# Graph attention streams: one PSUM bank for the weights, five or four for the slot sums, and an earlier place for two of the weighing steps

## The chip, the cores and the metric

The kernel runs on one core of a Trainium2 chip. The metric is the device time of one execution in microseconds; lower is better. A run's time is compared with others of the same kernel; the median of three runs is given.

## The reference

Two layers of a graph network over 6250 nodes with 256 features and 106250 edges (50000 random pairs in both directions, and a loop at each node), sorted by the node they lead to:

```
x = x + gat0(xn, edges) + mix0(xn)      # xn = layernorm(x)
x = x + moe0(layernorm(x))
x = x + gat1(xn, edges) + mix1(xn)      # gat1: two attention rounds, 4 heads, then 1
x = x + moe1(layernorm(x))
```

The change touches the three attention rounds (8, 4 and 1 heads). Each of them is

```
e     = leaky_relu(a_src[src] + a_dst[dst])
alpha = exp(e - max of e over the edges with this dst) / their sum
out   = sum over the edges with this dst of alpha * h[src]
```

## The kernel before

**Tiling.** The edges lie in slots of 256, which belong to one block of 128 nodes each; a slot has two units of 128 edges. There are 464 slots and 928 units, the same in all three rounds. Eight slots, 16 units, are a group; a round is a stream of 58 groups. `stream_sync`, `stream_gpsimd`, `stream_vector`, `stream_tensor` and `stream_scalar` issue it, one for each engine, each in an order written out by hand; semaphores join them. The mixers, the experts and the preparation of the edges lie outside the streams, but for `Out1`, the output part of the second layer's mixer, whose steps are hooked in between the steps of the second stream (`side.after_scores`, `side.before_carry` with L1970, `side.before_reference`, `side.after_weigh3` with L1987 and L1989, and so on). In the first and third stream `Alone` does nothing there. `Out1` uses PSUM bank 3.

**One group.** GpSimd gathers the row h[src] of each of 128 edges with one indirect DMA a unit (L978) into a ring of 48 units, three groups; it waits for `slot_mm` of the slot that used the place before. For group k, which is one ahead of the group g = k - 1 whose rows are weighed and summed:

- `expand` (TensorE, L1157) brings a_dst to the edges by one-hot matmuls, made by ScalarE's `one_hot` (L1252, L1254).
- `scores` (VectorE, L1008 to L1013) adds a_src and takes the leaky relu. `turn` (TensorE, L1165) transposes the scores, `turned` (ScalarE, L1258) copies them.
- `runs` (VectorE, L1020, L1022) takes running maxima along the edges of a node. `edges` (TensorE, L1169, L1170) brings the ends of the units into one row; `carry` (VectorE, L1030 to L1046) joins them over the units of the group; `cols` (TensorE, L1175) turns the result back; `reference` (VectorE, L1052 to L1056) subtracts the maximum.
- `weights` (ScalarE, L1264) takes exp; `back` (TensorE, L1181, L1182) transposes the result into a PSUM bank of the weights (`BK_W`, two of them, taken in turn); ScalarE copies them (L1266), takes the factor of the rescaling (L1267) and signals `r_ready`.

For group g the weights are there:

- `weigh(g, q)` (VectorE, L1065) multiplies the four units of quad q in place by the weights it reads from `BK_W`, and signals `m_ready`.
- `spread(g, q)` (ScalarE, L1241, L1244) makes the 0/1 matrices of edges against nodes, `Sr`, for the quad, and signals `s_ready`.
- `quad(g, q)` (TensorE, L1194) multiplies them with the rows: for each of its two slots two matmuls into one PSUM bank. The sums of the slots take banks 0, 1 and 2 in turn, and a slot waits until the sum three slots back has been taken (L1191, `slot_added`). The last matmul of a slot signals `slot_mm`.
- `add(s)` (VectorE, L1087) adds the slot's sum to the block's output; `rescale` (L1074) comes before a group's first sum.

**Orders.** VectorE in one turn of the loop: `scores(k)`, weigh 0, the last two sums of the group before, `rescale`, `runs(k)`, weigh 1, sums 0 and 1, `carry(k)`, weigh 2, sums 2 and 3, `reference(k)`, weigh 3, sums 4 and 5. TensorE: `turn(k)`, quad 0, `edges(k)`, quad 1, `cols(k)`, quad 2, `expand(k + 1)`, `back(k)`, quad 3. An engine issues strictly in its order, and each step waits for what it needs. SP brings the masks of group k + 2 when `reference` of group k has signalled `x_ready`. fp32 matmuls stand in the trace as two instructions each, so a quad has eight.

Of the kernel before, what the change touches and what calls it, by code (L numbers as in the profile page):

```python
# [11 lines left out]
ALU = mybir.AluOpType  # L12
ACT = mybir.ActivationFunctionType
# [107 lines left out]
def program(nc, A, out):  # L121
    ctx = ExitStack()
    with ctx:
# [23 lines left out]
        ident = sb("ident", [128, 128])  # L147
# [15 lines left out]
        banks = [ctx.enter_context(nc.psum_tensor(f"ps{i}", [128, 512], F32)) for i in range(8)]  # L163
# [705 lines left out]
        def mix0_gpsimd(e):  # L869
# [24 lines left out]
        assert AR.at <= 25608  # L894
        r_ready, s_ready, m_ready, slot_mm, slot_added, y_clear, den_ready, split_ready, scaled = [
            sem(n) for n in ("r_ready", "s_ready", "m_ready", "slot_mm", "slot_added", "y_clear", "den_ready", "split_ready", "scaled")]
        BK_AD, BK_T, BK_W = banks[4], banks[5], banks[6:8]

        AR.reset()
        Yflat = AR.take(NB * 264)  # L900
# [2 lines left out]
        Sr = AR.take(8, 128)  # L903
# [27 lines left out]
        def g_units(L, u, n):  # L931

            a = u % 48 * L.YW
            return Gflat[:, a:a + n * L.YW].rearrange("p (u h d) -> p u h d", u=n, h=L.H)
# [62 lines left out]
        def stream_vector(e, L, walk, side):  # L997
# [60 lines left out]
            def weigh(g, q):  # L1058

                K = L.k0 + g  # L1060
                if q == 0:
                    e.wait_ge(r_ready, K + 1)
                G = g_units(L, 16 * g + 4 * q, 4).rearrange("p u h d -> p (u h) d")[:, :, 0:D]
                w = BK_W[K % 2][:, 4 * H * q:4 * H * q + 4 * H].unsqueeze(2).to_broadcast([128, 4 * H, D])
                e.tensor_tensor(G, G, w, ALU.mult).then_inc(m_ready, 1)  # L1065

            def rescale(g):
# [9 lines left out]
            def add(s, at):  # L1077
                n = L.s0 + s
                if at is None:
                    at = walk.to(s, YW, WORDS)  # L1080
                o = Yv[:, bass.ds(at, YW)]
                e.wait_ge(slot_mm, n + 1)
                if s % 8 == 0:
                    e.wait_ge(scaled, L.k0 + s // 8 + 1)
                else:
                    e.wait_ge(slot_added, n)
                e.tensor_tensor(o, banks[n % 3][:, 0:YW], o, ALU.add).then_inc(slot_added, 1)  # L1087

            x = ADS[:, 0:NB * H].rearrange("p (b h) -> p b h", h=H)
            parts = AD3[:, 0:NB * L.TS].rearrange("p (b n) -> p b n", n=L.TS)  # L1090
# [9 lines left out]
            for g in range(-1, NG2):  # L1100
                k = g + 1
                more = k < NG2
                if more:
                    scores(k)
                side.after_scores(e, k)
                if g >= 0:
                    weigh(g, 0)
                    if g >= 1:
                        add(8 * g - 2, None)
                        add(8 * g - 1, None)  # L1110
                    at = rescale(g)
                side.before_runs(e, k)
                if more:
                    runs(k)
                if g >= 0:
                    weigh(g, 1)
                if g >= 0:
                    add(8 * g, at)
                    add(8 * g + 1, None)
                side.before_carry(e, k)  # L1120
                if more:
                    carry(k)
                if g >= 0:
                    weigh(g, 2)
                    add(8 * g + 2, None)
                    add(8 * g + 3, None)
                side.before_reference(e, k)
                if more:
                    reference(k)
                if g >= 0:  # L1130
                    weigh(g, 3)
                side.after_weigh3(e, k)
                if g >= 0:
                    add(8 * g + 4, None)
                    add(8 * g + 5, None)
# [8 lines left out]
        def stream_tensor(e, L, walk, side):  # L1144
# [32 lines left out]

            def back(k):
                e.wait_ge(ex_ready, L.k0 + k + 1)
                w = BK_W[(L.k0 + k) % 2]  # L1180
                e.transpose(w[:, 0:P], B2[0:P, :], ident[0:P, 0:P])  # L1181
                e.matmul(w[:, 128:128 + H], OHROW[0:1, :], DD[0:1, 0:H], start=True, stop=True).then_inc(al_ps, 1)  # L1182

            def quad(g, q):
                Q = 4 * (L.k0 + g) + q
                e.wait_ge(s_ready, Q + 1)
                e.wait_ge(m_ready, Q + 1)
                for s in range(8 * g + 2 * q, 8 * g + 2 * q + 2):
                    n = L.s0 + s
                    if n >= 3:  # L1190
                        e.wait_ge(slot_added, n - 2)  # L1191
                    for i in range(2):
                        u = 2 * s + i
                        t = e.matmul(banks[n % 3][:, 0:YW], Sr[:, u % 8, :], GV[:, u % 48, :], start=(i == 0), stop=(i == 1))  # L1194
                    t.then_inc(slot_mm, 1)

            e.wait_ge(split_ready, L.i + 1)
# [32 lines left out]
        def stream_scalar(e, L, side):  # L1230
# [28 lines left out]

            def weights(k):  # L1260
                K = L.k0 + k
                w = BK_W[K % 2]
                e.wait_ge(x_ready, K + 1)
                e.activation(B2[0:P, :], B2[0:P, :], ACT.Exp).then_inc(ex_ready, 1)  # L1264
                e.wait_ge(al_ps, K + 1)
                e.activation(g_units(L, 16 * k, 16)[:, :, :, D], w[:, 0:P].rearrange("p (u h) -> p u h", h=H), ACT.Copy)  # L1266
                e.activation(RR[:, 0:H], w[:, 128:128 + H], ACT.Exp).then_inc(r_ready, 1)  # L1267

            one_hot(0, 0)
            one_hot(0, 1)  # L1270
# [1435 lines left out]
```

## Time and profile before

| what | value |
|---|---|
| median of 3 runs | 6557.96 us (6548.13 to 6566.23) |
| span of the profiled execution, first to last instruction | 6525.8 us |
| what lies around the span in that execution | not among the rows |
| mean granted TensorE clock, share of full speed | 0.796 |
| first, second, third stream, us from the span's start | about 580 to 1915, 2700 to 4235, 4340 to 5715 |
| busy: TensorE matmuls, VectorE, ScalarE, GpSimd | 66%, 54%, 49%, 50% |

How to read it: busy time counts an engine's own instructions, not its waits, register work or DMA issue. "Idle before" is the time the engine stood still just before an instruction, and behind the arrow stands what ended it: an engine with the line of the instruction that released it, "issue" where the profile shows nothing that it waited for, "remote" where the semaphore moved at that moment but no instruction's end is near it. The start of a TensorE row is recorded, its end is modelled. PEclk is the clock granted to TensorE, as a share of 2.4 GHz; its two levels are 1.2 and 2.4 GHz. A row by stretch has: the stretch and its length in us; busy us and instructions of PE (TensorE's matmuls), PEld (its weight loads), DVE (VectorE), ACT (ScalarE) and POOL (GpSimd); PEclk; the DMA engines' busy share; GB/s.

### The profile page before, as it was taken

What the parts mean: (1) busy time and instruction counts of PE and PEld (TensorE: products, weight loads), DVE (VectorE), ACT (ScalarE), POOL (GpSimd) and SP (SyncE); (2) the same over time, 40 slices, a digit from 0 to 9 for tenths busy, and PEclk for the clock granted to TensorE, in tenths of its full rate; (3) what the DMA queues carried; (4) which work ended last, traced back from release to release, by engine and by line L of the source; (5) the groups of instructions that cost most, each with busy time, mean ns of one, the idle gap of its engine ahead of it and who ended that gap; (6) DMA issues with size and microseconds to landing.
All of it is one profiled execution on the core that took longest, in us unless ns stands there. A gap on an engine that the chain in (4) does not pass through costs nothing.

```text
span 6525.8 us, 75215 instructions
## 1 busy us (share of the span) xinstructions
PE 4307.6 (66%) x17795; PEld 2999.8 (46%) x17795; DVE 3511.9 (54%) x10013; ACT 3189.4 (49%) x7093; POOL 3265.5 (50%) x3443
## 2 busy tenths in 40 slices
PE   2896565666653696677676766645555555589798
PEld 2554444444432584355555554434444444433455
DVE  4376565656566437566666666655554545552211
ACT  1365555555542223466666666545555555544222
POOL 0125666666655535355555555546666666501222
PEclk9997777767775798777877778777776677799999
DMA  3292444444431333233333333334444444310110
GB/s 101 63 281 79 122 122 122 121 122 121 123 100 54 103 110 113 80 105 103 105 100 106 101 102 102 96 109 114 113 114 115 113 115 112 97 65 23 33 36 26
DMA packets 347491, 659.78 MB, mean 101 GB/s; under 512 B 78834, under 2 KB 196608, under 8 KB 346664
## 3 DMA queue, kind: packets, MB, share of 16 engines
q0 software_dynamic: 156336, 433.43, 24.1%
q1 hardware_dynamic: 190732, 221.55, 11.6%
q8 instruction: 164, 2.69, 0.2%
q14 instruction: 259, 2.12, 0.1%
HBM read 540.63 MB, written 115.42 MB: 101 GB/s over the span
## 4 chain that ended last, share of the span: by engine, by line
PE 26%; ACT 14%; another core or an unknown queue 13%; issue 7%; DVE 6%; POOL 2%; DMA 0%; DVEq 0%; SPq 0%; POOLq 0%; ACTq 0%
PE ps L1194 6%; ACT AR L1241 4%; PE ps L2560 3%; PE ps L2541 3%; PE ps L2249 2%; ACT AR L1254 2%; ACT AR L1252 2%; ACT AR L1244 2%; PE ps L2046 1%; POOL D_sx L1635 1%; PE ps L1678 1%; PE ps L1669 1%; PE ps L2261 1%; DVE AR L1087 1%
## 5 line engine op out<-in xcount | busy, mean ns | idle before, releaser
L978 POOL DMA_INDIRECT AR<-D_z,SRCI x1856 | 1758.9, 948 | 1231.6 <-issue 490.6
L1194 PE MATMUL ps<-AR 128*128 128x264 f32 (+2 forms) x5568 | 1923.5, 504 | 280.5 <-issue 133.0
L1194 PEld LDWEIGHTS ps<-AR 128*128 128x128 f32 x5568 | 1345.4, 254 | 641.6 <-issue 181.6
L978 POOL DMA_INDIRECT AR<-D_h,SRCI x904 | 865.7, 958 | 458.1 <-issue 242.8
L1241 ACT ACTIVATE AR<-iota_n,NREL 128x128 f32<-128x128 f32 x2784 | 880.9, 389 | 205.4 <-remote 143.9
L1087 DVE TENSOR_TENSOR AR<-ps,AR 128x264 f32 (+2 forms) x1392 | 589.5, 424 | 544.9 <-remote 228.7
L1065 DVE TENSOR_TENSOR AR<-AR,ps 128x1024 f32<-128x1024 f32 x696 | 836.8, 1202 | 6.3 <-ACT AR L1267 6.0
L1244 ACT ACTIVATE AR<-AR,ones 128x512 f32<-128x512 f32 x696 | 502.2, 722 | 22.6
L1266 ACT ACTIVATE AR<-ps 128x128 f32<-128x128 f32 (+2 forms) x174 | 51.1, 294 | 864.9 <-remote 728.3
L1254 ACT ACTIVATE AR<-AR,ones 128x1024 bf16<-128x1024 bf16 x348 | 399.5, 1148 | 11.3
L1252 ACT ACTIVATE AR<-AR,iota_p 128x1024 bf16<-128x1024 bf16 x348 | 394.7, 1134 | 20.3 <-DMA AR<-D_rel 20.3
L1175 PE MATMUL ps<-ones,AR 1*128 1x1 f32 (+2 forms) x696 | 83.1, 219 | 437.8 <-DVE AR L1046 327.6
L1008 DVE TENSOR_REDUCE AR<-ps 128x128 f32<-128x384 f32 (+2 forms) x174 | 64.7, 372 | 509.9 <-remote 496.7
L1165 PE MATMUL ps<-ident,AR 128*128 128x128 f32 (+2 forms) x174 | 60.6, 348 | 382.7 <-DVE AR L1013 335.9
L1052 DVE SCALAR_TENSOR_TENSOR AR<-AR,ps 128x128 f32<-128x128 bf16 (+2 forms) x174 | 60.3, 346 | 457.8 <-remote 431.7
L1175 PEld LDWEIGHTS ps<-ones,AR 1*128 1x128 f32 (+2 forms) x696 | 68.1, 158 | 501.0 <-DVE AR L1046 364.6
L2472 POOL DMA_INDIRECT out<-X x57 | 56.8, 997 | 332.5 <-DVE X L2508 322.3
L1157 PE MATMUL ps<-AD,AR 128*128 x2784 | 165.0, 174 | 83.6 <-issue 43.9
L1165 PEld LDWEIGHTS ps<-ident,AR 128*128 128x128 f32 (+2 forms) x174 | 23.4, 134 | 426.4 <-issue 420.9
L1181 PE MATMUL ps<-ident,AR 128*128 128x128 f32 (+2 forms) x174 | 57.0, 327 | 241.9 <-ACT AR L1264 220.3
L2541 PE MATMUL ps<-AR 128*128 x912 | 200.8, 381 | 18.2 <-ACT AR L2525 18.2
L1264 ACT ACTIVATE AR<-AR 128x128 f32<-128x128 f32 (+2 forms) x174 | 53.3, 306 | 322.9 <-DVE AR L1056 242.1
(437 smaller groups left out, 7814.2 us busy)
## 6 DMA issues: line engine op xcount, KB each, us to landing
AR<-D_rel SPq DMA_DIRECT2D x348, 256.0 KB
D_sx<-AR SPq DMA_DIRECT2D x8, 6370.0 KB
AR<-D_z,SRCI POOLq DMA_INDIRECT x1856
AR<-D_h,SRCI POOLq DMA_INDIRECT x928
D_y<-AR SPq DMA_DIRECT2D x106, 128.0 KB, 1.7
AR<-in_L_ffn_Wd SPq DMA_DIRECT2D x8, 1024.0 KB
AR<-D_mask SPq DMA_DIRECT2D x58, 128.0 KB
D_h<-AR SPq DMA_DIRECT2D x49, 132.0 KB
```

What stands on the lines that cost most here:

```text
L978: e.indirect_dma_start(out=GV[:, u % 48, :], out_offset=None, in_=D_row[L.i], in_offset=bass.IndirectOffsetOnAxis(ap=SRCI[:, u:u + 1], axi ...
L1065: e.tensor_tensor(G, G, w, ALU.mult).then_inc(m_ready, 1)
L1087: e.tensor_tensor(o, banks[n % 3][:, 0:YW], o, ALU.add).then_inc(slot_added, 1)
L1157: t = e.matmul(BK_AD[:, 3 * H * u:3 * H * u + 3 * H], OHr[v][:, 128 * (u % 8):128 * (u % 8) + 128], AD3[:, at], start=True, stop=True)
L1175: t = e.matmul(BK_T[0:P, 384 + i:385 + i], ROW[0:1, i, 0:P], ones[0:1, 0:1], start=True, stop=True)
L1194: t = e.matmul(banks[n % 3][:, 0:YW], Sr[:, u % 8, :], GV[:, u % 48, :], start=(i == 0), stop=(i == 1))
L1241: t = e.activation(w[:, i, :], iota_n[:, :], ACT.Abs, bias=NREL[:, u:u + 1])
L1244: e.activation(w[:, :, :], w[:, :, :], ACT.Relu, bias=ones[:, 0:1], scale=-1.0).then_inc(s_ready, 1)
L1252: e.activation(OHr[v], RBr[n % 2], ACT.Abs, bias=iota_p[:, 0:1], scale=-1.0).then_inc(*ac.up())
L1254: e.activation(OHr[v], OHr[v], ACT.Relu, bias=ones[:, 0:1], scale=-1.0).then_inc(oh_ready, 1)
L2541: t = e.matmul(ps[:, 0:256], rH2[q % 2][:, m, 128 * i:128 * i + 128], Wd[:, m, bass.ds(at, 256)], start=(m == 0), stop=(m == 7))
L2560: t = e.matmul(banks[2 + n % 4][:, 0:w], W1[:, k, 128 * m:128 * m + 128], rxt3[q % 2][:, k, 0:w], start=(k == 0), stop=(k == 1))
```

## The change

The weights keep one bank, 6, for all groups. Bank 7 goes to the sums: the slots of the first and third stream take banks 0, 1, 2, 3 and 7 in turn, those of the second 0, 1, 2 and 7 (bank 3 belongs to the side work). A slot waits for the sum as many slots back as there are banks, and the first slots of a stream wait for none. In VectorE's order weigh 2 moves from behind `carry` to behind weigh 1, ahead of sums 0 and 1; weigh 3 moves from behind `reference` to behind `carry`, where weigh 2 was, ahead of sums 2 and 3. The orders of the other engines, all instructions and their sizes stay.

```diff
--- before.py
+++ after.py
@@ -894,7 +894,13 @@
         assert AR.at <= 25608
         r_ready, s_ready, m_ready, slot_mm, slot_added, y_clear, den_ready, split_ready, scaled = [
             sem(n) for n in ("r_ready", "s_ready", "m_ready", "slot_mm", "slot_added", "y_clear", "den_ready", "split_ready", "scaled")]
-        BK_AD, BK_T, BK_W = banks[4], banks[5], banks[6:8]
+        BK_AD, BK_T, BK_W = banks[4], banks[5], banks[6]
+        SUMS = ((0, 1, 2, 3, 7), (0, 1, 2, 7), (0, 1, 2, 3, 7))
+
+        def sum_of(L, s):
+
+            return banks[SUMS[L.i][s % len(SUMS[L.i])]][:, 0:L.YW]
+
 
         AR.reset()
         Yflat = AR.take(NB * 264)
@@ -1061,7 +1067,7 @@
                 if q == 0:
                     e.wait_ge(r_ready, K + 1)
                 G = g_units(L, 16 * g + 4 * q, 4).rearrange("p u h d -> p (u h) d")[:, :, 0:D]
-                w = BK_W[K % 2][:, 4 * H * q:4 * H * q + 4 * H].unsqueeze(2).to_broadcast([128, 4 * H, D])
+                w = BK_W[:, 4 * H * q:4 * H * q + 4 * H].unsqueeze(2).to_broadcast([128, 4 * H, D])
                 e.tensor_tensor(G, G, w, ALU.mult).then_inc(m_ready, 1)
 
             def rescale(g):
@@ -1084,7 +1090,7 @@
                     e.wait_ge(scaled, L.k0 + s // 8 + 1)
                 else:
                     e.wait_ge(slot_added, n)
-                e.tensor_tensor(o, banks[n % 3][:, 0:YW], o, ALU.add).then_inc(slot_added, 1)
+                e.tensor_tensor(o, sum_of(L, s), o, ALU.add).then_inc(slot_added, 1)
 
             x = ADS[:, 0:NB * H].rearrange("p (b h) -> p b h", h=H)
             parts = AD3[:, 0:NB * L.TS].rearrange("p (b n) -> p b n", n=L.TS)
@@ -1114,21 +1120,19 @@
                     runs(k)
                 if g >= 0:
                     weigh(g, 1)
-                if g >= 0:
+                    weigh(g, 2)
                     add(8 * g, at)
                     add(8 * g + 1, None)
                 side.before_carry(e, k)
                 if more:
                     carry(k)
                 if g >= 0:
-                    weigh(g, 2)
+                    weigh(g, 3)
                     add(8 * g + 2, None)
                     add(8 * g + 3, None)
                 side.before_reference(e, k)
                 if more:
                     reference(k)
-                if g >= 0:
-                    weigh(g, 3)
                 side.after_weigh3(e, k)
                 if g >= 0:
                     add(8 * g + 4, None)
@@ -1177,21 +1181,19 @@
 
             def back(k):
                 e.wait_ge(ex_ready, L.k0 + k + 1)
-                w = BK_W[(L.k0 + k) % 2]
-                e.transpose(w[:, 0:P], B2[0:P, :], ident[0:P, 0:P])
-                e.matmul(w[:, 128:128 + H], OHROW[0:1, :], DD[0:1, 0:H], start=True, stop=True).then_inc(al_ps, 1)
+                e.transpose(BK_W[:, 0:P], B2[0:P, :], ident[0:P, 0:P])
+                e.matmul(BK_W[:, 128:128 + H], OHROW[0:1, :], DD[0:1, 0:H], start=True, stop=True).then_inc(al_ps, 1)
 
             def quad(g, q):
                 Q = 4 * (L.k0 + g) + q
                 e.wait_ge(s_ready, Q + 1)
                 e.wait_ge(m_ready, Q + 1)
                 for s in range(8 * g + 2 * q, 8 * g + 2 * q + 2):
-                    n = L.s0 + s
-                    if n >= 3:
-                        e.wait_ge(slot_added, n - 2)
+                    if s >= len(SUMS[L.i]):
+                        e.wait_ge(slot_added, L.s0 + s - len(SUMS[L.i]) + 1)
                     for i in range(2):
                         u = 2 * s + i
-                        t = e.matmul(banks[n % 3][:, 0:YW], Sr[:, u % 8, :], GV[:, u % 48, :], start=(i == 0), stop=(i == 1))
+                        t = e.matmul(sum_of(L, s), Sr[:, u % 8, :], GV[:, u % 48, :], start=(i == 0), stop=(i == 1))
                     t.then_inc(slot_mm, 1)
 
             e.wait_ge(split_ready, L.i + 1)
@@ -1259,12 +1261,11 @@
 
             def weights(k):
                 K = L.k0 + k
-                w = BK_W[K % 2]
                 e.wait_ge(x_ready, K + 1)
                 e.activation(B2[0:P, :], B2[0:P, :], ACT.Exp).then_inc(ex_ready, 1)
                 e.wait_ge(al_ps, K + 1)
-                e.activation(g_units(L, 16 * k, 16)[:, :, :, D], w[:, 0:P].rearrange("p (u h) -> p u h", h=H), ACT.Copy)
-                e.activation(RR[:, 0:H], w[:, 128:128 + H], ACT.Exp).then_inc(r_ready, 1)
+                e.activation(g_units(L, 16 * k, 16)[:, :, :, D], BK_W[:, 0:P].rearrange("p (u h) -> p u h", h=H), ACT.Copy)
+                e.activation(RR[:, 0:H], BK_W[:, 128:128 + H], ACT.Exp).then_inc(r_ready, 1)
 
             one_hot(0, 0)
             one_hot(0, 1)
```

## Rows read from the trace of the kernel before

**Rows 1.** Busy time by stretch: the first, second and third stream.
```profile
580.00:1915.00 1335.00, 806.30 (x3295) 577.89 (x3295) 816.07 (x1886) 733.38 (x1595) 859.18 (x898) 0.74 0.43 120
2700.00:4235.00 1535.00, 1029.28 (x4405) 761.21 (x4404) 934.90 (x2587) 960.12 (x2095) 874.42 (x923) 0.77 0.37 103
4340.00:5715.00 1375.00, 763.49 (x3338) 551.49 (x3339) 682.45 (x1911) 732.65 (x1620) 869.07 (x918) 0.71 0.40 111
```

**Rows 2.** L1008, `scores`, in the first and third stream: starts, and releasers of its waits.
```profile
L1008 DVE TENSOR_REDUCE AR<-ps x58: 547/557/559, 587.5 to 1904.8; 128x128 f32<-128x384 f32 x58
...
  remote: 171.6, 41
...
L1008 DVE TENSOR_REDUCE AR<-ps x58: 197/207/209, 4341.4 to 5694.2; 128x16 f32<-128x48 f32 x58
...
  remote: 211.5, 30
```

**Rows 3.** Costliest groups, GpSimd's gathers, first, second and third stream.
```profile
L978 POOL DMA_INDIRECT AR<-D_h,SRCI x898 | 859.6, 957 | 455.7 <-issue 241.3 <-remote 165.5 <-PE ps L1194 48.9
...
L978 POOL DMA_INDIRECT AR<-D_z,SRCI x923 | 875.3, 948 | 635.1 <-PE ps L1194 313.4 <-issue 240.9 <-remote 80.8
...
L978 POOL DMA_INDIRECT AR<-D_z,SRCI x918 | 869.3, 947 | 475.5 <-issue 245.7 <-remote 198.3 <-PE ps L1194 31.4
```

**Rows 4.** VectorE in order of time, two groups of the first stream (start, duration).
```profile
1217.96 0.43 DVE L1087 TENSOR_TENSOR AR<-ps,AR 128x264 f32 x1 [3.92 <-PE ps L1194]
...
1223.23 1.20 DVE L1065 TENSOR_TENSOR AR<-AR,ps 128x1024 f32<-128x1024 f32 x1
...
1234.42 0.56 DVE L1008 TENSOR_REDUCE AR<-ps 128x128 f32<-128x384 f32 x1 [5.45 <-remote]
...
1241.48 0.27 DVE L1030 COPY AR<-ps 1x128 f32<-1x128 f32 x1
...
1244.72 1.20 DVE L1065 TENSOR_TENSOR AR<-AR,ps 128x1024 f32<-128x1024 f32 x1
...
1252.11 0.36 DVE L1052 SCALAR_TENSOR_TENSOR AR<-AR,ps 128x128 f32<-128x128 bf16 x1 [5.21 <-remote]
```

**Rows 5.** GpSimd in order of time, the same stretch.
```profile
1223.07 0.94 POOL L978 DMA_INDIRECT AR<-D_h,SRCI  x1 [2.56 <-remote]
...
1234.76 0.94 POOL L978 DMA_INDIRECT AR<-D_h,SRCI  x1 [2.00 <-PE ps L1194]
...
1252.42 0.94 POOL L978 DMA_INDIRECT AR<-D_h,SRCI  x1 [2.67 <-remote]
```

**Rows 6.** TensorE's matmuls in order of time, the same stretch.
```profile
1244.86 0.60 PE L1175 MATMUL ps<-ones,AR 1*128 1x1 f32 x4 [2.16 <-DVE AR L1046]
1246.03 3.04 PE L1194 MATMUL ps<-AR 128*128 128x264 f32 x8 [0.57 <-issue]
```

**Rows 7.** L1052, `reference`: us and times TensorE's release ended its wait, by stream.
```profile
  remote: 81.0, 20
...
  remote: 181.3, 38
...
  remote: 169.4, 26
```

**Rows 8.** Costliest groups, TensorE: L1194 in the three streams, then L1175 in the first.
```profile
L1194 PE MATMUL ps<-AR 128*128 128x264 f32 x1808 | 661.5, 526 | 89.9 <-issue 45.6 <-DVE AR L1065 20.3 <-ACT AR L1244 17.1
...
L1194 PE MATMUL ps<-AR 128*128 128x260 f32 x1821 | 578.9, 474 | 61.4 <-ACT AR L1244 31.3 <-issue 14.0 <-DVE AR L1087 13.7
...
L1194 PE MATMUL ps<-AR 128*128 128x257 f32 x1846 | 659.8, 517 | 126.3 <-issue 71.5 <-ACT AR L1244 43.7 <-DVE AR L1087 7.9
...
L1175 PE MATMUL ps<-ones,AR 1*128 1x1 f32 x228 | 44.7, 296 | 217.1 <-DVE AR L1046 180.6 <-issue 36.5
```

**Rows 9.** Costliest groups, VectorE's side work in the second stream.
```profile
L1970 DVE SCALAR_TENSOR_TENSOR AR<-ps,AR 128x256 f32<-128x256 f32 x49 | 23.4, 477 | 15.5 <-PE ps L2006 8.1 <-remote 7.3
...
L1987 DVE TENSOR_TENSOR X<-X,ps 128x256 f32<-128x256 f32 x49 | 20.6, 420 | 66.9 <-issue 33.9 <-PE ps L2035 30.1 <-remote 3.0
```

## The prediction

> **What bounds the kernel now.** I began with the page and the busy times by stage. The three streams fill 1335, 1535 and 1375 us of a span of 6525.8 us, and no engine is above 68% in any of them [rows 1]. Outside them the change alters no instruction. So I looked for the beat of a stream. The instance rows of the first VectorE step of a group give it: 58 groups whose first and last start at 587.5 and 1904.8 us are 23.1 us apart in the first stream, and in the third (4341.4 to 5694.2) 23.7 [rows 2]; the second's 1535 us are 26.5 a group [rows 1].
>
> The third stream is the telling one. VectorE has 682.45 us of work there against 816.07 in the first [rows 1], 2.3 us a group less, much of it in `carry`, yet its group is no shorter. VectorE's work is not what sets the beat of these two. GpSimd's rows come near it: busy time and the idle time put down to "issue" are 859.6 + 241.3 us for 898 gathers, 1.23 us each, or 19.6 us for the 16 of a group; the other idle time is 165.5 + 48.9 us, 3.7 a group. In the third stream 1.21 us each and 198.3 + 31.4 us give 19.4 + 4.0; in the second the pauses are 313.4 + 80.8 us, 6.8 a group [rows 3]. The gathers stop because they want rings of rows back, which `slot_mm` gives.
>
> Next I read two groups of the first stream in order of time. VectorE stands still three times in them: 3.92 us before the second sum at 1217.96, 5.45 us before `scores` at 1234.42, 5.21 us before `reference` at 1252.11 [rows 4]. GpSimd pauses three times in the same stretch, 2.56, 2.00 and 2.67 us [rows 5]. Each VectorE wait is for TensorE, and longer than TensorE's own rows explain: the `cols` matmuls end by their row at 1245.46 and quad 2 behind them at 1249.07 [rows 6], but `reference`, which needs `cols` alone, starts at 1252.11. TensorE's finished work becomes visible late while gathers are under way, and comes free about when they pause. The reader is to see that most gaps of VectorE are not lack of work on TensorE but this lateness. How common the three are: `reference` waits for TensorE in 20 groups of the first stream and 26 of the third [rows 7], `scores` in 41 and 30 [rows 2].
>
> **Five (four) banks for the sums.** A slot's matmul waited for the sum three slots back. The idle time that TensorE spends before L1194 for L1087 is 13.7 us in the second stream, 7.9 in the third, and in the first under 17.1, the smallest releaser printed [rows 8]. All of it would be under 39 us. Below, the gain is nothing, since most of TensorE's earlier start is eaten by late visibility. I take a quarter-odd, 8 us. A loss I exclude: no bank is shared anew by engines at one time; back(k) writes the one weights bank only after reference(k), which now stands behind weigh 3.
> The Trainium skill (Perfetto Trace Analysis, Optimizing Tensor Performance, Matmuls) says that independent matmul groups should rotate through PSUM banks so that emptying one overlaps filling the next. By that rule alone the whole wait of under 39 us would go; the rows show the rotation already short of binding.
>
> **Weigh 2 goes from behind `carry` to before the first two sums.** One weigh is 1.20 us [rows 4]. What it frees: quad 2 no longer waits for it. In the second of the two groups `carry` gives way to weigh 2 at 1244.72 [rows 4], and quad 2 starts at 1246.03 while `cols` is over at 1245.46 [rows 6]: 0.57 us. TensorE's idle time for L1065 in the first stream is 20.3 us [rows 8]. The gain lies between 0 and 0.57 x 116 = 66 us for the first and third streams; I take 0.3 us in half of the groups, 17 us.
> What it costs: `carry` starts 1.2 us later wherever VectorE wasn't waiting before it. In about half of the groups it was (3.92 us at 1217.96 [rows 4], cover enough). In the others (`carry` at 1241.48 waits for nothing [rows 4]) `cols` is 1.2 us later, and queued behind `cols` on TensorE are quad 2, `expand` and `back`. There the wait before `reference` covers it: 5.21 us. I take 0; if visibility moves with `cols`, the price is 1.2 x 57 = +68 us.
>
> **Weigh 3 goes from behind `reference` to before the next sums.** In groups whose `reference` waits, it is done in the wait, and VectorE, which after 1252.11 [rows 4] has its next steps ready, is 1.2 us ahead: weigh 0, quad 0 and `runs` come 1.2 us earlier. What is late next is the second sum (3.92 us of wait [rows 4]). If that wait ends with a pause of the gathers, the 1.2 us are lost in it; if it ends with its own matmul, they are kept. So 0 to 1.2 x 57 pairs = 68 us; I take half, 34 us. In the other groups weigh 2 plays the same part inside the wait of 1217.96, and the next wait (5.45 us) takes what it gains: 0. ScalarE's exp and `back` wait for `reference`, which is no later there, as one weigh before it replaces another. No DMA moves; SP's masks wait for x_ready, GpSimd for `slot_mm`, and neither is later.
>
> **The second stream** has side work in the same order. Weigh 2 now precedes L1970 too, whose whole wait is 15.5 us in 49 [rows 9], so there is almost no cover before it: L1970 and `carry` are 1.2 us late in every group, 1.2 x 58 = +70 us if nothing hides it. Behind them stands the wait of `reference`, 181.3 us in 38 of 58 groups [rows 7]. Uncovered are some 20 groups: +24 us. After `reference` the freed 1.2 us fall into the wait of L1987 (66.9 us in 49, 1.4 each [rows 9]): no gain. Below nothing isn't excluded, as the pauses of 6.8 us a group may shrink: 0 to +70, I take +24.
>
> **Sum.** -8 - 17 - 34 + 24 = -35 us against the profiled execution: 6525.8 to about 6491. The span lies 32 us (0.5%) under the median of the runs, and no row shows what lies around it; I take the same step from the median: 6558 - 35 = 6523 us.
>
> **The rivals.**
> A, a pause drops out. The first and third streams look locked: three pauses to two groups. 57 pairs, one pause of 2.0 to 2.7 us less in each, about 120 us: 6438. For it: freed VectorE time comes right after a release, when completions are prompt (`scores` at 1234.42 is followed by `carry` at 1241.48 with no wait named [rows 4]). Against: 2.3 us less work in the third stream dropped none.
> B, slower: `carry` becomes the bound. Its place is L1175 behind L1046, where TensorE already idles 180.6 us in the first stream [rows 8]. Price 1.2 us where VectorE arrives at `carry` unhindered: +68 and +70, less 17 + 34 + 8 freed and some of the cover left, about +60: 6618. It decides once more than half of the `reference` waits move with `cols` instead of ending at a pause. For it: the second stream has no cover before `carry`; against: the waits are 3 to 5 us, 1.2 is little.
> The Trainium skill (TensorE: Matmul & The Clock Gate, Why this matters for your kernels) warns that idle gaps between bursts halve TensorE's clock. The granted clock is 0.71 in the third stream and 0.77 in the busier second [rows 1], which agrees; by that rule a longer gap before `cols` would make B dearer, by what no row tells.
> C, nothing moves: the gathers and their pauses set the beat and every 1.2 us sinks into another wait, as between the first and third streams: 6558. The banks not binding at all belongs here.
>
> **How the numbers follow.** Forecast 0.40 (its own range 6483 to 6553, from twice the gain to hardly any), A 0.15, B 0.22, C 0.23. About 0.3% (20 us) is what a measurement can tell from no change. Faster takes A and four fifths of the forecast, 0.47; same C and the rest, 0.31; slower B, 0.22. The range takes in A's 6438 and goes up to just short of B's 6618; half of A and of B may lie beyond: 6435 to 6615.
>
> **What would show it.** Idle time before L1194 for sums near 0 (banks); quad 2 starting when `cols` ends; `reference` waits shorter by 1.2 us in the first and third streams, and the waits before the second sum shorter too; GpSimd's pauses fewer (A), the same (C) or longer (B); TensorE's idle time for L1046 longer by up to 60 us a stream in B. I'd be wrong if the waits before `reference` stay as long as now with `carry` later.

## The result, and the profile after

The changed kernel needs 6599.07 us (median of 20 runs, 6563.23 to 6625.98), the kernel before 6547.66 in the 20 runs beside them (6510.41 to 6588.46). The ratio of after to before is 1.0073, with a 95% interval of 1.0054 to 1.0091: slower by some 48 us, where the forecast was 35 us faster. The new time lies inside the range given, but on the side of rival B. The profiled execution of after took 6616.12 us, its span is 6614.1; that is 17 us above its median, and the one of before shown above lay 20 us under its own, so the two spans overstate the loss.

The busy times by stretch of the changed kernel answer to [rows 1] (columns: stretch, its length, then busy us and instructions of PE, PEld, DVE, ACT and POOL, the granted clock, the DMA share, GB/s):

```profile
580.00:1930.00 1350.00, 806.86 (x3286) 592.24 (x3287) 813.73 (x1871) 729.37 (x1584) 861.03 (x900) 0.72 0.44 119
2700.00:4310.00 1610.00, 1049.20 (x4496) 767.09 (x4496) 955.62 (x2643) 978.83 (x2146) 881.51 (x928) 0.78 0.37 99
4400.00:5800.00 1400.00, 735.55 (x3358) 535.89 (x3356) 698.06 (x1916) 736.23 (x1626) 879.31 (x928) 0.73 0.41 111
```

No engine has more to do: over the whole span TensorE's matmuls are busy 4282 us against 4308 before, VectorE 3524 against 3512. The first line of the answer for `scores` in each stream gives its length as in [rows 2], from the first start to the last:

```profile
L1014 DVE TENSOR_REDUCE AR<-ps x58: 547/557/559, 590.4 to 1928.1; 128x128 f32<-128x384 f32 x58
...
L1014 DVE TENSOR_REDUCE AR<-ps x58: 347/358/359, 2744.5 to 4298.8; 128x64 f32<-128x192 f32 x58
...
L1014 DVE TENSOR_REDUCE AR<-ps x58: 197/208/209, 4420.6 to 5781.8; 128x16 f32<-128x48 f32 x58
```

From 590.4 to 1928.1 are 1338 us, then 1554 and 1361, against 1317, about 1511 and 1353 of before. All three look longer. Only the second is, as the profiles from set 4 below will show; the profile of before shown above came from other conditions. The costliest groups that answer to [rows 8] and [rows 3] (TensorE's quads by stream, then `cols` in the first, then the gathers by stream):

```profile
L1196 PE MATMUL ps<-AR 128*128 128x264 f32 x1808 | 673.3, 536 | 42.0 <-DVE AR L1071 19.3 <-issue 12.3 <-ACT AR L1246 10.2
...
L1179 PE MATMUL ps<-ones,AR 1*128 1x1 f32 x228 | 47.3, 308 | 242.5 <-issue 149.0 <-DVE AR L1052 93.5
...
L1196 PE MATMUL ps<-AR 128*128 128x260 f32 x1812 | 570.8, 470 | 54.3 <-ACT AR L1246 23.3 <-issue 15.9 <-DVE AR L1093 8.6
...
L1196 PE MATMUL ps<-AR 128*128 128x257 f32 (+1 forms) x1866 | 639.8, 501 | 67.3 <-ACT AR L1246 61.2 <-issue 4.6 <-DVE AR L1071 1.1
```

```profile
L984 POOL DMA_INDIRECT AR<-D_h,SRCI x904 | 865.2, 957 | 478.7 <-issue 243.1 <-remote 160.6 <-PE ps L1196 74.2
...
L984 POOL DMA_INDIRECT AR<-D_z,SRCI x928 | 881.5, 950 | 747.3 <-PE ps L1196 353.8 <-issue 243.3 <-remote 81.5
...
L984 POOL DMA_INDIRECT AR<-D_z,SRCI x928 | 879.3, 948 | 536.7 <-issue 250.7 <-remote 172.7 <-PE ps L1196 64.5
```

The change does what it says. TensorE's idle time ahead of the quads falls from 89.9 to 42.0 us in the first stream and from 126.3 to 67.3 in the third. In the first it comes back ahead of `cols` (217.1 to 242.5 us), and the gathers pause no less: 160.6 + 74.2 = 235 us in the first stream, where before had 214, and 435 in the second, where before had 394.

### The profile page after: what moved, and what is told of

Read it like the earlier page. It is cut to its first block, busy times and chain, and to the rows that moved or that the text cites. A ratio compares the mean times of both kernels' runs of the same rounds, so it can differ in the third digit from the quotient of the medians.

```text
span 6614.1 us, 75215 instructions
## 1 busy us (share of the span) xinstructions
PE 4282.1 (65%) x17795; PEld 2993.8 (45%) x17795; DVE 3524.4 (53%) x10013; ACT 3187.7 (48%) x7093; POOL 3267.8 (49%) x3443
## 4 chain that ended last, share of the span: by engine, by line
PE 24%; another core or an unknown queue 12%; ACT 12%; DVE 9%; issue 9%; POOL 2%; DVEq 1%; DMA 1%; SPq 0%; POOLq 0%; ACTq 0%
PE ps L1196 5%; ACT AR L1243 4%; PE ps L2561 3%; PE ps L2542 3%; PE ps L2250 2%; DVE AR L1093 2%; ACT AR L1256 2%; ACT AR L1254 2%; ACT AR L1246 2%; PE ps L2047 2%; PE ps L1679 1%; POOL D_sx L1636 1%; PE ps L1670 1%; PE ps L2262 1%
## 5 line engine op out<-in xcount | busy, mean ns | idle before, releaser
L1071 DVE TENSOR_TENSOR AR<-AR,ps 128x1024 f32<-128x1024 f32 x696 | 823.5, 1202 | 7.6 <-ACT AR L1268 7.3
```

## The experiments

Eighteen runs of twelve kernels follow, in five sets; the kernels of a set share a chip and the runs of before beside them. The sets differ in something that no kernel controls. What the traces show of it is how late TensorE's completions become visible: not at all in set 2, some 3 us in the others. So a ratio belongs to its own set, and each set begins with the time of before in it.

### Set 1: the change in parts (before 6547.22 us)

**order_alone**: the new order on the old banks.

```diff
-                if g >= 0:
+                    weigh(g, 2)
                     add(8 * g, at)
...
-                    weigh(g, 2)
+                    weigh(g, 3)
                     add(8 * g + 2, None)
...
-                if g >= 0:
-                    weigh(g, 3)
```

> VectorE's order of the changed kernel on the banks of the kernel before (two for the weights, three for the sums). Theory (the 1.2 us of weigh 2 ahead of carry go through to the period, most of all in the second stream): slower than before by 40 to 65 us, the second stream by about 45. Rival (the new banks do it: a TensorE that runs ahead holds up the turn and the scores): within 15 us of before.

Measured: 1.0017 (0.9997 to 1.0037), some 11 us. The theory fails; the number fits the rival, but banks_alone, next, speaks against its reason.

**banks_alone**: the old order, four banks for the sums in streams 1 and 3.

```diff
+        SUMS = (4, 3, 4)
...
-                    if n >= 3:
-                        e.wait_ge(slot_added, n - 2)
+                    if s >= SUMS[L.i]:
+                        e.wait_ge(slot_added, L.s0 + s - SUMS[L.i] + 1)
```

> The order of before, with a fourth bank for the sums in streams 1 and 3. Theory (the order costs, the banks give back little): 0 to 20 us faster than before. Rival (the banks cost): slower by 15 to 30 us, all of it in streams 1 and 3.

Measured: 0.9977 (0.9953 to 1.0001), some 15 us faster if anything. A fourth bank in streams 1 and 3 is no loss.

**w2_behind_carry** and **w2_behind_in_s2**: the changed kernel with weigh 2 back behind `carry`, in all streams and in the second alone (there the `if` lines read `L.i != 1` and `L.i == 1`).

```diff
                     weigh(g, 1)
-                    weigh(g, 2)
                     add(8 * g, at)
...
                 if g >= 0:
+                    weigh(g, 2)
                     weigh(g, 3)
```

> The changed kernel with weigh 2 put back behind carry (carry, weigh 2, weigh 3, sums 2 and 3, reference) in all streams; the banks of the change stay. Theory (weigh 2 ahead of carry costs it): within 15 us of before. Rival (weigh 3 ahead of the sums and reference, or the banks, cost it): slower than before by 35 to 50 us, as the changed kernel is.

> The changed kernel with weigh 2 put back behind carry in the second stream alone. Theory: the second stream gives back its 44 us, so the kernel is slower than before by 0 to 20 us. Rival (place of weigh 2 is not the cause): slower by 35 to 50 us.

Measured: 0.9997 (0.9981 to 1.0014) and 0.9998 (0.9981 to 1.0015). With weigh 2 behind `carry` in the second stream alone nothing of the main result's loss is there. Weigh 3 ahead of `reference` and the new banks are in both kernels, so they don't cost it here. But this set doesn't show yet that weigh 2 does: the changed kernel itself was not in it, and order_alone, which has weigh 2 ahead too, hardly lost. I took that for an interplay with the banks, which the next set was to test.

### Set 2: completions on time (before 5761.37 us)

**changed_again** is the changed kernel itself. **s2_three_sums** and **three_sums** cut `SUMS` to `(0, 1, 2)` in the second stream and in all. **w2_ahead_in_s2_only** is w2_behind_in_s2 with the two conditions swapped.

> The changed kernel itself, beside the three others of this set, on their chip. It was 1.0073 of before. Theory (new order and new banks together cost, in the second stream alone): 1.005 to 1.009 again. Rival (the first set of runs put a chance of the chip or of its memory on it): under 1.003, as order_alone had 1.0017.

> The changed kernel with three banks for the sums in the second stream instead of four; the order and the five banks of the other streams stay. Theory (weigh 2 ahead of carry costs 45 us only where a fourth bank lets quad 1 run ahead of sum 8g): slower than before by 0 to 20 us. Rival (the single bank for the weights, or the five banks of streams 1 and 3, make the difference to order_alone): slower by 35 to 50 us, as changed.

> The changed kernel with weigh 2 ahead of carry only in the second stream, behind it in streams 1 and 3. Theory (all of the loss is the second stream's): slower than before by 35 to 50 us. Rival (streams 1 and 3 lose as well): slower by 15 to 30 us.

> The changed kernel with three banks for the sums in all streams; the weights keep one bank. Theory (the single weight bank costs nothing): as order_alone, slower than before by 0 to 25 us. Rival (back now meets the readers of the one weight bank): slower by over 35 us.

Measured: 0.9955 (0.9942 to 0.9969), 0.9962 (0.9949 to 0.9976), 0.9979 (0.9969 to 0.9988) and 0.9962 (0.9948 to 0.9975). Theories and rivals fell alike: here before needs 786 us less than in set 1, and the same changed kernel is faster than before, by some 26 us. The profile shows what differs. These are, of changed_again and for the first stream, the answer for `scores` with what ended its waits, and then the groups of the gathers and of `reference`:

```profile
L1014 DVE TENSOR_REDUCE AR<-ps x58: 545/547/558, 574.6 to 1700.8; 128x128 f32<-128x384 f32 x58
...
  PE ps L1161: 0.9, 1
```

```profile
L984 POOL DMA_INDIRECT AR<-D_h,SRCI x904 | 868.6, 961 | 277.4 <-issue 233.2 <-PE ps L1196 26.6 <-DMA AR<-D_h,SRCI 16.8
...
L1058 DVE SCALAR_TENSOR_TENSOR AR<-AR,ps 128x128 f32<-128x128 bf16 x57 | 19.9, 349 | 1.1 <-PE ps L1179 1.1
```

The gathers' issue is 868.6 + 233.2 us for 904 of them, 19.5 us a group, and the group takes (1700.8 - 574.6) / 57 = 19.8: here GpSimd's issue is the bound of the first stream. Its other pauses are 44 us (277.4 - 233.2) against 235 in the profile of after, `reference` waits 1.1 us in all, `scores` 0.9. Side by side in time are first changed_fourth (a set with late completions) with `expand` on TensorE, `scores` that waits for it, and a gather behind a pause, then changed_again with `cols`, `reference`, `expand` and `scores`:

```profile
1218.33 0.63 PE L1161 MATMUL ps<-AD,AR 128*128 x16
...
1224.74 0.56 DVE L1014 TENSOR_REDUCE AR<-ps 128x128 f32<-128x384 f32 x1 [5.26 <-remote]
...
1225.09 0.95 POOL L984 DMA_INDIRECT AR<-D_h,SRCI  x1 [2.72 <-remote]
```

```profile
1231.07 0.60 PE L1179 MATMUL ps<-ones,AR 1*128 1x1 f32 x4 [2.57 <-DVE AR L1052]
1233.03 0.34 DVE L1058 SCALAR_TENSOR_TENSOR AR<-AR,ps 128x128 f32<-128x128 bf16 x1
1233.48 0.70 PE L1161 MATMUL ps<-AD,AR 128*128 x16
1235.27 0.55 DVE L1014 TENSOR_REDUCE AR<-ps 128x128 f32<-128x384 f32 x1
```

In the first, `expand` ends by its row at 1218.96 and `scores` gets it 5.8 us later, while GpSimd pauses. In the second it ends at 1234.18 and `scores` starts 1.1 us after, behind VectorE's own work. I counted this over the first stream: of TensorE's rows that raise a semaphore, matched to the next recorded event within 10 us, 739 of 753 have it within 0.1 us of the row's end in changed_again, 198 of 724 in before_itself of set 4, where the mean is 2.97 us late. That mean is too high where an event was not recorded; with only the events that come before the next row of the same semaphore it is 2.2 us (488 rows).

The waits themselves need no events, only the rows, so I took them from all twenty profiles: the time between the end of `expand`'s row and the start of `scores`, as far as VectorE stood idle in it. Its mean over the first stream is 2.6 to 3.3 us in the sixteen profiles with late completions and at most 0.02 us in the four of set 2. VectorE's and ScalarE's completions are not late: from the end of `scores` on VectorE to `turn` on TensorE the same measure is at most 0.14 us in every profile, from ScalarE's exp to `back` 0.03. And the late ones do end in pauses of the gathers: of the 56 waits over 1 us before `scores` and `reference` in the first stream of before_itself, 54 end inside a pause of GpSimd of over 1 us, though such pauses fill 17% of the time (changed_fourth: 56 of 58).

The late condition is not the only difference between the sets. The granted clock is 0.85 to 0.86 in set 2 and 0.79 to 0.81 in the others. By the rows it can explain a part at most: TensorE's matmuls are busy 4062 us in changed_again and 4282 in changed_fourth, 219 us of a difference of 880 between the two spans. Of these 880 us, 818 lie in the three streams, where the gathers run beside TensorE's steps. No run here takes the clock and the lateness apart.

Of the parts, three_sums shows no worth of the banks here (0.9962 against 0.9955, inside both intervals), and w2_ahead_in_s2_only that weigh 2's new place in streams 1 and 3 gives about 14 us of the 26 (the two intervals touch at 0.9969).

### Set 3: late again (before 6541.52 us)

**changed_third**, **s2_three_sums_b** and **three_sums_b** are the kernels of set 2 once more. **before_longer_by_one** is before with idle work for VectorE:

```diff
+                if g >= 0:
+                    e.tensor_reduce(SPARE[:, 0:8], iota_n[:, :].unsqueeze(1).to_broadcast([128, 8, 128]), AX.X, ALU.add)
                 side.before_carry(e, k)
```

> The changed kernel once more. On one chip it was slower than before by 0.7%, on another, where before needs 5761 us and hardly a completion of TensorE comes late, faster by 0.45%. Theory (the sign goes with the chip: a gain where completions come on time, none or a loss where they come late): 0.994 to 0.997 if before needs about 5760 us here, 1.002 to 1.009 if it needs about 6550. Rival (the sign is a chance of one placement or of one set of runs): 0.994 to 1.000 with before at 6550 as well.

> Three banks for the sums in the second stream. With before at about 6550 us: theory (the loss needs the new place of weigh 2 and the fourth bank of the second stream together) 1.000 to 1.003; rival (the place of weigh 2 alone, and order_alone was a lucky set) 1.005 to 1.009. With before at about 5760: 0.996 again.

> Three banks for the sums in all streams, one for the weights: the order alone, in other banks. With before at about 6550 us: theory as order_alone, 1.000 to 1.003; rival 1.005 to 1.009. With before at about 5760: 0.996 again, since banks do nothing there.

> The kernel before, with one added reduction of 128x1024 elements on VectorE (about 1.1 us, its result unused) ahead of carry in all 57 groups of each stream; nothing is taken away elsewhere. Where the path through carry is the bound of the period it costs up to 174 times 1.1 us, 190 us. Theory: where completions come late (before at 6550) the period follows them and the second stream's share alone goes through, 30 to 70 us; where they come on time (5760) the gathers' issue hides it but in the second stream, 10 to 40 us. Rival (carry is the bound in every stream): 120 to 190 us.

Measured: 1.0094 (1.0073 to 1.0115), 1.0117 (1.0096 to 1.0138), 1.0089 (1.0068 to 1.011), and 1.0048 (1.0019 to 1.0076) for the longer before, some 31 us. In the sets so far the sign goes with the lateness, with one set on time. The interplay with the banks is refuted: with three banks the order loses as with five. The sizes scatter, though: s2_three_sums_b is 15 us slower than changed_third, three_sums_b 9 us faster, which no account of the banks explains. And the added reduction, up to 190 us if `carry` bounded every stream, costs a sixth of that: in its profile the first and third streams take 1343 and 1365 us (from the starts of `scores`), against 1343 and 1364 in changed_third, so 57 reductions in each sink without a trace. (The kernel before has no profile in this set; in set 4 its first and third streams take what the changed kernel's do.) The second takes 1567, in an execution that was the slowest of its set (6648 us against a median of 6578).

### Set 4: all on one chip (before 6542.66 us)

**changed_fourth**, **order_alone_b**, **w2_behind_in_s2_b** repeat what their names say, and **before_itself** is the kernel before.

> The changed kernel beside the three others of this set, on their chip. With before near 6545 us: the theory that the loss belongs to every chip where completions come late gives 1.005 to 1.010 again; the rival that it belongs to some of these chips (not to the one of the first set) allows 0.999 to 1.003.

> The order of the change on the banks of before, again. With before near 6545 us and changed_fourth near 1.008: theory (the order loses by itself; the first set's 1.0017 was its chip) 1.005 to 1.010; rival (one bank for the weights is needed for the loss, as three_sums_b has it and this has not) 1.000 to 1.003.

> The changed kernel with weigh 2 behind carry in the second stream, again. Its first stream is the changed kernel's, instruction for instruction, and yet took 1318 us from the first to the last scores in the first set, against 1338 and 1343 in the changed kernel's own runs. Theory (chip): the first stream takes what changed_fourth's does, within 8 us, and the whole is 1.002 to 1.006. Rival (no chip effect): first stream 1318, whole 1.000.

> The kernel before, to have its profile from the same chip: ratio 1.000. First stream 1317 us from the first to the last scores as in the profile shown, if the chip doesn't set it; 1340 if it does.

Measured: 1.0087 (1.0053 to 1.0121), 1.0072 (1.0044 to 1.0099), 1.0029 (1.0002 to 1.0056), 1.0012 (0.9988 to 1.0036). The order alone has the loss; its 1.0017 belonged to set 1. With weigh 2 back behind `carry` in the second stream most of it goes, 41 us of 61 by the medians: the intervals of 1.0087 and 1.0029 just overlap, but eleven of the twelve times of w2_behind_in_s2_b lie below the lowest of changed_fourth. The starts of `scores` in the three streams, first before_itself, then changed_fourth:

```profile
L1008 DVE TENSOR_REDUCE AR<-ps x58: 548/557/559, 588.5 to 1926.3; 128x128 f32<-128x384 f32 x58
...
L1008 DVE TENSOR_REDUCE AR<-ps x58: 348/358/359, 2740.5 to 4194.3; 128x64 f32<-128x192 f32 x58
...
L1008 DVE TENSOR_REDUCE AR<-ps x58: 197/207/209, 4315.7 to 5676.5; 128x16 f32<-128x48 f32 x58
```

```profile
L1014 DVE TENSOR_REDUCE AR<-ps x58: 547/557/558, 590.7 to 1929.9; 128x128 f32<-128x384 f32 x58
...
L1014 DVE TENSOR_REDUCE AR<-ps x58: 347/357/359, 2745.9 to 4305.6; 128x64 f32<-128x192 f32 x58
...
L1014 DVE TENSOR_REDUCE AR<-ps x58: 197/207/209, 4427.5 to 5788.3; 128x16 f32<-128x48 f32 x58
```

The first stream takes 1338 and 1339 us, the third 1361 and 1361: the change moves them by nothing. The second takes 1454 and 1560. The same subtraction gives 1341, 1539 and 1360 for order_alone_b, and 1340, 1466 and 1361 for w2_behind_in_s2_b. These second streams overstate the difference, since the profiled executions are not median ones (6511.2 us for before_itself with a median of 6551.62; 6623.02 for changed_fourth with 6603.32). With that taken off, 46 us are left, near the loss by the medians. The first stream's 1338 to 1341 us in all four, against 1316 to 1319 in the four kernels of set 1 and 1317 in the profile that the prediction read, shows that this stream's time belongs to the set and not to the kernel.

The groups of the second stream in the same two profiles, before_itself and changed_fourth: gathers, the side work ahead of `carry`, the sum into X behind `reference`, and `reference`:

```profile
L978 POOL DMA_INDIRECT AR<-D_z,SRCI x928 | 881.8, 950 | 647.4 <-issue 252.4 <-PE ps L1194 232.9 <-remote 93.4
...
L1970 DVE SCALAR_TENSOR_TENSOR AR<-ps,AR 128x256 f32<-128x256 f32 x49 | 23.6, 482 | 82.1 <-remote 67.2 <-PE ps L2006 14.7
...
L1987 DVE TENSOR_TENSOR X<-X,ps 128x256 f32<-128x256 f32 x49 | 20.6, 421 | 93.3 <-issue 62.1 <-PE ps L2035 24.1 <-remote 7.1
...
L1052 DVE SCALAR_TENSOR_TENSOR AR<-AR,ps 64x128 f32<-64x128 bf16 x57 | 19.4, 341 | 23.4 <-remote 22.7 <-issue 0.7
```

```profile
L984 POOL DMA_INDIRECT AR<-D_z,SRCI x928 | 882.4, 951 | 752.1 <-PE ps L1196 335.6 <-issue 249.9 <-remote 97.8
...
L1971 DVE SCALAR_TENSOR_TENSOR AR<-ps,AR 128x256 f32<-128x256 f32 x49 | 23.3, 476 | 6.7 <-remote 5.7 <-issue 1.0
...
L1988 DVE TENSOR_TENSOR X<-X,ps 128x256 f32<-128x256 f32 x49 | 20.6, 421 | 165.2 <-issue 89.4 <-PE ps L2036 62.6 <-remote 13.1
...
L1058 DVE SCALAR_TENSOR_TENSOR AR<-AR,ps 64x128 f32<-64x128 bf16 x57 | 19.5, 343 | 88.1 <-remote 87.5 <-issue 0.7
```

In this profile of before the wait ahead of L1970 (82.1 us) covers weigh 2: 6.7 are left. The loss comes behind it. `reference` waits 65 us more, the sum into X 72 us more, and the gathers' pauses grow by 107 us (232.9 + 93.4 to 335.6 + 97.8), which is the whole difference of the two second streams; in the first the pauses stay, 231 and 232 us. My reading, which no run shows by itself: a step that starts a little later can miss a pause and has its completion seen at the next.

TensorE in the first stream shows where freed time goes. These are `cols` in before_itself and in changed_fourth:

```profile
L1175 PE MATMUL ps<-ones,AR 1*128 1x1 f32 x232 | 45.2, 295 | 190.2 <-DVE AR L1046 129.2 <-issue 61.0
```

```profile
L1179 PE MATMUL ps<-ones,AR 1*128 1x1 f32 x228 | 46.9, 306 | 231.6 <-issue 147.3 <-DVE AR L1052 84.3
```

The idle time ahead of quad 2 falls from 22 us to nothing and that for the sums inside the quads from 15 us to nothing, and the idle time ahead of `cols` grows by 41.

### Set 5: which chain of the second stream (before 6566.56 us)

Two chains stand behind the new place of weigh 2. The side work ahead of `carry` (L1971) feeds a turn, the product with Wo and the sum into X (L1988); `carry` feeds `cols`, `reference` and `back`. Each kernel delays one of them, in the second stream alone. **side_first**:

```diff
                 side.before_carry(e, k)
+                if g >= 0 and L.i == 1:
+                    weigh(g, 2)
                 if more:
                     carry(k)
```

**carry_first**:

```diff
-                side.before_carry(e, k)
                 if more:
                     carry(k)
+                if L.i == 1:
+                    if g >= 0:
+                        weigh(g, 2)
+                    side.before_carry(e, k)
```

> The changed kernel with weigh 2 between the side work of the second stream (the attention update ahead of carry) and carry, in the second stream alone: carry is 1.2 us late as in the change, the side work is not. Where before needs about 6545 us: theory O (the side chain over the update, its turn, the product with Wo and the sum into X is what the second stream waits for) 0.999 to 1.003; theory C (carry, cols and reference are it) 1.006 to 1.010. Where before needs 5760: 0.995 to 0.998 by both.

> The changed kernel with carry ahead of weigh 2 and of the side work in the second stream alone (carry, weigh 2, side work, weigh 3): carry is as early as in before or earlier, the side work 3.5 us late. Where before needs about 6545 us: theory O 1.006 or more, since the side chain is later still; theory C 0.995 to 1.002. Where before needs 5760: 0.995 to 1.003.

Measured: 1.0014 (0.9987 to 1.0041) and 1.0067 (1.0043 to 1.009). By the times the loss goes with the side work: with L1971 ahead of weigh 2 it is gone as far as the interval tells, though `carry` is as late as in the change, and with `carry` early and L1971 late it is there. The changed kernel itself is not in this set. The profiles don't settle it. Their second streams take 1538 us in side_first and 1515 in carry_first, the other way round, in executions 41 us above and 6 below their medians. And `reference` waits 87.5 us in that stream of side_first, as in the change, and 46.5 in carry_first, so its wait does follow a late `carry`, whether or not the stream pays for it. I hold the side chain for likely, on two intervals that don't overlap, and not for shown. The runs name the chip of this set by the same number as that of set 2, and yet before took 6567 us here and 5761 there; so the lateness isn't fixed to that number.

## Why the prediction was wrong

**What bounds the kernel.** The reading held: late completions and pauses of the gathers, not work, make the beat. In set 2, where the lateness is absent, before needs 786 us less; what part the higher granted clock there has in that is not told apart.

**The sum.** The forecast was -35 us, the set 4 profiles and medians give some +50. Of the 85 us between, 59 are gains that didn't come (8, 17 and 34), and some 26 are the second stream's, which cost twice the 24 us. Neither step alone would have given the result.

**Banks, -8 us.** TensorE's wait for the sums went as forecast, to nothing that a row names in the first stream. What that is worth can't be told from 0: 1.0094 against 1.0089 and 0.9955 against 0.9962 with three banks throughout, while banks_alone had 0.9977 and s2_three_sums_b lost 15 us more than the change. The intervals reach 8 to 14 us to either side, so a gain of 8 us would hardly be seen.

**Weigh 2 from in front of quad 2, -17 us.** The rows were misread: TensorE's 20.3 us for L1065 [rows 8] stand ahead of quad 0, which waits for weigh 0, and are 19.3 after. What stands ahead of quad 2 is 22 us put down to "issue", and it did go to nothing. So the size was near, the wait was freed, and where completions are late the stream gained nothing by it.

**Weigh 3 inside the wait of `reference`, -34 us.** Where completions are late this gave nothing either: streams 1 and 3 keep their times to 3 us in set 4. The failed choice is the half that I took for kept, between 0 and 68 us. The text named the other end itself, that a wait which ends with a pause of the gathers swallows the gain. It swallows all. In the first stream the wait before the second sum, 8g+1, does fall as forecast, from 82 us in before_itself to 48 in changed_fourth, and that of `reference` by 21; the waits before sum 8g+5 and before the second of the two sums behind weigh 0 grow by 29 and 16 us, that before `scores` by 8. Where completions are on time, 26 us came in all, and 14 of them by weigh 2 in these streams, near the 17. That the 26 us come near the forecast of 35 is partly luck: it is a condition that its profile didn't have, with the gathers' issue as the bound of the first stream.

**The second stream, +24 us.** This step came out some 26 us too low, and it carries the loss. I took the 1.2 us as covered in 38 of 58 groups by the wait of `reference` [rows 7] and counted only the rest, though L1970's own delay was named in the same sentence. Its chain ends in L1988, not in `reference`, and no row of `reference` covers it; set 5 makes that chain likely as the one that pays. Measured: some 50 us, inside the bounds of 0 and 70 given; putting weigh 2 back takes 41 us off in set 4. Besides, the profile read was of one condition of that stream (1511 us, `reference` waiting 181.3 us for TensorE in 38 groups); another of the same kernel has 1454 us, and `reference` waits 22.7 in 5.

**The rivals.** A didn't happen. B had the size and the side right and the place wrong: it had `cols` behind `carry` lose in streams 1 and 3 too. TensorE's idle time before `cols` rises by 41 us in the first stream of set 4, but the part that waits for `carry` falls, from 129.2 to 84.3, and before_longer_by_one adds 1.1 us ahead of `carry` there and the stream doesn't notice. C describes the first and third streams exactly. So the result is C in the first and third streams, and in the second the loss that B had priced, likely with the side work carrying it.

**The sign that I named for an error** was `reference` waiting as long as now with `carry` later. In the first stream its wait falls from 135.1 us in before_itself to 113.9 in changed_fourth, about 0.4 us a group and not 1.2, and in the second it grows. GpSimd's pauses, the other sign, are the same in the first stream (C) and longer in the second (B).

**Open:** what makes TensorE's completions late in some sets, and what sets apart set 1, where order_alone lost 11 us and not 46. An estimate says where to look: a median less what a profile of the set shows outside the second stream leaves for that stream 1526 us in before (with banks_alone's profile) and 1535 in order_alone in set 1, and 1486 in before and 1540 in the change in set 4. By this estimate before was slower there in set 1, rather than the new order faster. The changed kernel itself didn't run in that set, nor a kernel with fewer or smaller gathers in any, so that the gathers hold the completions back is argued from the 54 of 56 waits and not tried. The spread of 30 us either way between executions lies in the second stream by these profiles; what starts one in the shorter or the longer of its beats is open too.

## What to carry to other kernels

Before a stall is given a price, find out what ends it. If waits end when another engine pauses, not when the work waited for is done, time freed ahead of them can be worth nothing (here 59 us were forecast and none came), and time added can be free too (114 reductions of 1.1 us in two streams); price both at the pause. When a step is moved ahead of several others, follow each chain behind it to its own last reader: a wait that covers one chain says nothing of its neighbour. And read two profiles of the kernel before from different runs, since one may show a beat that the next hasn't.

## What was not expected of the hardware

The same program had its TensorE events on time in one set and some 3 us late in the others, at 5761 and about 6550 us for the kernel before. The gathers' rows are alike in both: 961 and 957 ns each in the first stream. VectorE's and ScalarE's completions are on time in both; of these engines' steps only what waits for TensorE waits longer. The Trainium skill (Perfetto Trace Analysis, Tensor Engine Instruction (MATMUL, LD_WEIGHTS)) says that the end of a matmul's row is worked out and not observed, and that the semaphore is pushed after PSUM has acknowledged the data and is then propagated. The trace of set 2 agrees, with 0.03 us on the mean. That the reader can be some 3 us behind the row's end is no statement of the page, and the other sets show it.

The late condition shows in the recorded events as well. On the ten semaphores of the gathers the trace of changed_again holds 50,841 increments, that of changed_fourth, the same program, 11,046. The Trainium skill (DMA: Bandwidth & Descriptors, Why a DMA increments its semaphore by 16 and not by 1) says that each of 16 engines posts one for such a transfer; 2784 gathers would make 44,544, which only the first trace can hold; the ten serve 433 other transfers too. Whether the increments of the other were bunched or only not recorded, no run here tells.

Of the three streams two don't react to the change at all, to 3 us in 1340, while the middle one has been seen at 1454, 1511 and 1560 us under nearly the same instructions.
